# Moving TensorE's load of block numbers, and four of its steps, in a graph layer with a mixture-of-experts FFN

## What is computed

```
def _L0_gnn_ref(x, edge_index, weight, bias):
    summed = jax.ops.segment_sum(x[src], dst, num_segments=n)
    deg = jax.ops.segment_sum(jnp.ones_like(src, dtype=x.dtype), dst, num_segments=n)
    agg = summed / jnp.maximum(deg, 1.0)[:, None]
    out = jnp.concatenate([x, agg], axis=-1) @ weight
    out = out / jnp.linalg.norm(out, axis=-1, keepdims=True)
    return out + bias
...
def _L0_ffn_ref(h, gate_w, gate_b, w1, b1, w2, b2):
    logits = x @ gate_w + gate_b
    probs = jax.nn.softmax(logits, axis=-1)
    idx = jnp.argmax(probs, axis=-1)
    ...
    buf = jnp.zeros((E, C, D), dtype=h.dtype).at[idx, pos_safe].set(x, mode='drop')
    hmid = jax.nn.relu(jnp.einsum('ecd,edf->ecf', buf, w1) + b1[:, None, :])
    ybuf = jnp.einsum('ecf,efd->ecd', hmid, w2) + b2[:, None, :]
...
x = x + _L0_gnn_ref(_layernorm(x, axis=-1), edge_index, L0_gnn_weight, L0_gnn_bias)
x = x + _L0_ffn_ref(_layernorm(x, axis=-1)[None], ...)[0]
```

## Time and profile before

| | |
|---|---|
| timed runs | 1510.32, 1512.84, 1513.54 us; median 1512.84 |
| span of the profiled execution | 1742.4 us |
| TensorE, VectorE, GpSimd busy | 68%, 52%, 53% of the span |
| the main loop in the profiled execution | 156 to 1552 us |

### The profile page before, as it was taken

The page is one execution under the profiler, slowest core; times in us unless marked ns, Lnnn a source line. Parts: engine busy times, 40 slices in busy tenths (PEclk is TensorE's granted clock), DMA queues, the critical chain, the costliest instruction groups (busy, mean ns, idle before and its releaser), DMA issues.

```text
span 1742.4 us, 32300 instructions
## 1 busy us (share of the span) xinstructions
PE 1183.2 (68%) x6813; PEld 838.8 (48%) x6814; DVE 898.6 (52%) x3823; ACT 469.4 (27%) x1362; POOL 922.7 (53%) x939
## 2 busy tenths in 40 slices
PE   0105566677777777777777776877677777777785
PEld 0004444455555555555555554645455655554553
DVE  5753444455555545454555554554555545554443
ACT  2221111122222222222222322223222222233432
POOL 4136656656666656555656655565556665640110
PEclk9998676789999989998989998999998899888998
DMA  7736667554545444544445444444454544431111
GB/s 236 235 134 205 185 215 232 185 160 131 147 136 146 135 131 132 149 121 134 136 118 139 126 138 115 134 127 140 114 143 121 146 120 137 124 103 34 38 42 38
DMA packets 126810, 238.77 MB, mean 137 GB/s; under 512 B 21263, under 2 KB 85126, under 8 KB 126792
## 3 DMA queue, kind: packets, MB, share of 16 engines
q0 software_dynamic: 55808, 160.87, 32.7%
q1 hardware_dynamic: 70984, 77.72, 14.1%
HBM read 207.46 MB, written 39.29 MB: 142 GB/s over the span
## 4 chain that ended last, share of the span: by engine, by line
PE 28%; issue 19%; DVE 17%; another core or an unknown queue 11%; DVEq 10%; DMA 7%; ACT 4%; POOL 2%; SPq 2%; ACTq 0%; POOLq 0%
PE ps_q L684 10%; PE ps_h L747 5%; PE ps_b L766 5%; PE ps_a L738 3%; DVEq L1252 3%; DVEq L1060 2%; DMA ring<-parts_d,idx 2%; DVE sel L991 2%; PE ps_a L725 2%; DMA b_b<-in_L_ffn_b 2%; DMA out<-ys,node_i 1%; PE ps_t L755 1%; DVE acc L1000 1%; ACT cat_t L580 1%
## 5 line engine op out<-in xcount | busy, mean ns | idle before, releaser
L460 POOL DMA_INDIRECT ring<-parts_d,idx x784 | 763.0, 973 | 541.1 <-PE ps_q L684 277.9
L684 PE MATMUL ps_q<-ring,sel 128*128 128x256 bf16 x2928 | 506.0, 299 | 245.0 <-DMA ring<-parts_d,idx 96.7
L684 PEld LDWEIGHTS ps_q<-ring,sel 128*128 128x128 bf16 x2928 | 270.4, 106 | 416.8 <-issue 242.2
L766 PE MATMUL ps_b<-w_sb,hid_t 128*128 x864 | 264.6, 441 | 124.2 <-issue 71.2
L991 DVE SCALAR_TENSOR_TENSOR sel<-lane,block,dst_t 128x512 bf16<-128x512 bf16 x245 | 184.4, 753 | 197.4 <-issue 116.2
L766 PEld LDWEIGHTS ps_b<-w_sb,hid_t 128*128 128x128 f32 x864 | 169.6, 214 | 161.6 <-issue 141.5
L747 PE MATMUL ps_h<-w_sb,hid_t 128*128 x432 | 213.6, 622 | 5.7 <-ACT hid_t L583 5.7
L1000 DVE TENSOR_TENSOR acc<-acc,ps_q 128x257 f32 x245 | 103.3, 422 | 178.3 <-issue 57.3
L690 PE MATMUL ps_q<-ones_bf,sel 128*128 128x1 bf16 x976 | 170.8, 175 | 0.0
L738 PE MATMUL ps_a<-gw_sb,cat_t 128*128 128x256 f32 x416 | 136.3, 459 | 19.3 <-ACT cat_t L580 15.6
L604 ACT ACTIVATE hid_t<-ps_t,b_t 128x128 f32<-128x128 f32 x432 | 117.8, 382 | 55.5 <-remote 40.1
(11 more groups left out here) (180 smaller groups left out, 1296.1 us busy)
## 6 DMA issues: line engine op xcount, KB each, us to landing
w_sb<-in_L_ffn_w SPq DMA_DIRECT2D x32, 512.0 KB
ring<-parts_d,idx POOLq DMA_INDIRECT x784
disp_d<-row SPq DMA_DIRECT2D x1, 8450.0 KB
parts_d<-w_sb SPq DMA_DIRECT2D x6, 1344.0 KB, 5.8
xs<-disp_d SPq DMA_DIRECT2D x55, 130.0 KB
ys<-disp_d SPq DMA_DIRECT2D x55, 130.0 KB
b_b<-in_L_ffn_b SPq DMA_DIRECT2D x55, 128.0 KB
xb<-in_x SPq DMA_DIRECT2D x51, 128.0 KB
```

Of the source, the lines that this page charges most:

```text
L460: pool.indirect_dma_start(ring[:, (k % 2) * TQ + j, :], None, parts_d[:, :], bass.IndirectOffsetOnAxis(ap=idx[:, k * TQ + j:k * TQ + j + 1 ...
L684: mm = pe.matmul(ps[:, 0:D], sel[:, s, j, :], ring[:, (k % 2) * TQ + j, part * D:(part + 1) * D], start=(j == 0 and part == 0), stop=(j == ...
L766: last_ = pe.matmul(ps_b[:, 0:D], hid_t[:, j, :], w2_sb[:, j, ds(expert[0] * D, D)], start=(j == 0), stop=(j == JF - 1))
```

## The change

TensorE's load of the next trip's eight block numbers goes into eight spare registers, `next_regs`, and is moved from behind the first group of the last quad to behind the second half of the first FFN product in the third quad. A new step, `turn_quads`, copies them over at the trip's end. In `plan`, the first half of the first FFN product moves from behind group 2 to behind group 3 of the second quad; what follows in the third quad moves one group later each; `down` 0 and 1 move into the last quad; the transposes of the normalised row move from behind group 3 to behind group 2 of the last quad, and `down` 4 to 7 all stand behind group 3. Nothing else is changed.

```diff
+            next_regs = [pe.alloc_register(f"next_quad_blocks{i}") for i in range(2 * QS)]
...
                 def load_quads():
 
-                    pe.load(regs, qtab[0:1, ds(t * QS + QS, QS), :])
+                    pe.load(next_regs, qtab[0:1, ds(t * QS + QS, QS), :])
+
+                def turn_quads():
+                    for now, then in zip(regs, next_regs):
+                        pe.reg_mov(now, then)
...
                         [steps((node, linear, 0)),
                          steps((node, linear, 1)),
-                         steps((chunk, up, 0)),
-                         steps()],
-                        [steps((prev, counts), (chunk, up, 1)),
+                         steps(),
+                         steps((chunk, up, 0))],
+                        [steps((prev, counts)),
+                         steps((chunk, up, 1), (quads, load_quads)),
                          steps((chunk, hid_transposes, 0)),
-                         steps((chunk, hid_transposes, 1)),
-                         steps((chunk, down, (0, 1)))],
-                        [steps((quads, load_quads), (chunk, down, (2, 3))),
-                         steps((chunk, down, (4, 5))),
-                         steps((chunk, down, (6, 7))),
-                         steps((node, xl_transposes))]]
+                         steps((chunk, hid_transposes, 1))],
+                        [steps((chunk, down, (0, 1))),
+                         steps((chunk, down, (2, 3))),
+                         steps((node, xl_transposes)),
+                         steps((chunk, down, (4, 5, 6, 7)), (quads, turn_quads))]]
```

## The result

The changed kernel takes **1610.59 us** (median of 4 runs, 1608.28 to 1626.81); the kernel before, beside it, 1511.58 (4 runs, 1509.12 to 1513.54). The ratio is **1.067, with a 95% interval of 1.062 to 1.073**: 99 us slower. The forecast had the sign right and the size wrong by a factor of three (+32 us), and 1610 lies outside its range of 1485 to 1590.

The account below looks back on a forecast made before the run. The loop was taken to be bound by VectorE's chain, with ScalarE in its gaps. Load and other shifts counted 0, the new order 0.8 us in each of 40 trips: +32 us on 1512.84 gave 1545 us, range 1485 to 1590.

Parts of the forecast that it names:

- The bound: In the loop: VectorE's chain, with ScalarE in its gaps and TensorE a little ahead, sets the trip at 24.0 us.
- Part 1: TensorE's load behind the first FFN product: its 1.8 us stall falls to 0 to 0.2 us, taken as 0.
- Part 2: Transposes ahead of the last four second FFN products: TensorE waits 2.4 us for ScalarE, next quad starts 1.4 us later.
- s: Start of VectorE's selection for the extra visit, in nearly all trips in the last quad; 842.20 us in the trace before.
- X: End of the normalised row on ScalarE, put at a fixed 8.66 us after s.
- Part 3: How much of the next quad's 1.4 us delay reaches the chain, through the exponential: taken as 0.8 us a trip.
- Rival 3: The wait before the transposes lowers TensorE's clock: 1.9 us in 20 trips, 1583 us; chance 0.17, shared with an unhidden load.
- Rivals 1 and 2: First: TensorE's jitter sets the loop, the wait cushions it, 1459, chance 0.25; second: VectorE's chain hides everything, 1515, chance 0.11.
- The signs set down beforehand: Under 0.3 us idle after the load; 2 to 3 us before the transposes, some 100 in all; next quad X + 2.6 or later.

Follow-up runs that it names:

- e3: Changed kernel with the transposes of the normalised row put last in the trip again, the load left at its new place; 1514.0 us.
- e4: Changed kernel with two unread products issued ahead of TensorE's wait for the normalised row, in trips with a chunk; 1514.0 us.
- e6: Changed kernel with the transposes last again and VectorE's own load of block numbers moved to the trip's end, into spare registers; 1487.9 us.
- e9: Changed kernel, order untouched, with VectorE's own load of block numbers taken off its chain in two halves; 1477.6 us.
- e1: Kernel before with only TensorE's load moved behind the first FFN product, all other steps at their old places; 1526.1 us.
- e7: Kernel before with VectorE's own load of block numbers moved to the trip's end, nothing changed on TensorE; 1505.9 us.
- e2: Changed kernel's order of steps, but TensorE's load left in the last quad, into the old registers; 1528.1 us.
- e10: Kernel before with only TensorE's load moved, plus one unread product ahead of the wait for the normalised row; 1516.3 us.
- e5: Changed kernel with one unread product ahead of TensorE's wait for the normalised row, in trips with a chunk; 1527.4 us.

## Why the prediction was wrong in size

**The bound: right.** The chain of VectorE and ScalarE was put at 24.0 us a trip by taking the overstated waits out of the trace of before. Trips at full clock are 23.7 us (e3) and 24.05 us (e4). Taking work off that chain pays at full clock (0.33 us a trip in e6 against e3, 0.86 in e9 against e4); taking it off TensorE alone doesn't (e1; e6 against e7).

**Part 1, the load: right.** Hidden behind the first FFN product, nothing left at the new place, moves 0.18 us, and worth nothing by itself at full clock. The same 1.8 us came back at the transposes.

**Part 2, the new wait: right in place, too small in length.** The last visit's group started 2.57 us after the selection for the extra visit (837.40, the row below) and not 3.26, so TensorE stood at the transposes at s + 5.7 instead of s + 6.3; X came at s + 8.5 (8.66 predicted). The wait was 2.93 us in the trip shown and 3.1 in the mean, against 2.4. The row of VectorE for s, and of TensorE for that group, in the changed kernel:

```profile
837.40 0.75 DVE L996 SCALAR_TENSOR_TENSOR sel<-lane,block,dst_t 128x512 bf16<-128x512 bf16 x1 [0.32 <-issue]
```

```profile
839.97 0.49 PE L685 MATMUL ps_q<-ring,sel 128*128 128x256 bf16 x3
```

**Part 3, what reaches the chain: the step that failed.** The sum took X + 2.7 for the next quad and X + 5.85 for the exponential, both with TensorE at full clock behind the wait. In the changed kernel they are X + 4.8 and X + 8.4. At full clock (e4) they are X + 2.5 and X + 5.4 (the prediction's own terms, 0.3 + 0.35 + 1.9, make 2.55 and not 2.7): the mechanism of the order was right, with 0.28 us a trip (e4 against e3 at full clock) where 0.8 was taken, and its 32 us are not to be found in e4's time. What failed is the price of the products behind the wait: the sum had them all at full clock and put the clock's part at nothing. That part is 93 us: 3.03 us in each of 24 trips and 1.57 in 13 (the changed kernel less e4).

**Rival 3 is what happened.** It named the mechanism and the row that shows it: 2.16 us of idleness, then a stretch at a granted 0.51. It was given in half the trips, 1.9 us each, and a small chance. It should have been the forecast. The argument against it was that idle times of 1.8 us stand in the last quad of each trip already, and the loop is granted 0.92 all the same. Three things were missed there. A mean of 0.92 leaves room for a fall in some trips, and e2's and e7's rows show one behind 1.90 and 1.95 us. A wait of 2.4 us is longer than the 2.16 after which the fall had been seen, so the 1.8 say little about it. And the price is paid behind the gap: behind the old one stood two products and a quad's remainder with time to spare before X, behind the new one four products, the next quad and the transposes of cat, all in front of the exponential that the chain waits for. With rival 3's own numbers in nearly every trip, 40 x 1.9 = 76 us on top of the order's 0 to 32, the forecast would have been 1589 to 1621, and held the 1610.6. That this comes near is in part luck: the clock falls in 37 trips of 40, and where it falls for all of the 5 us it costs 3.0 us and not 1.9, as the groups and the transposes of cat are slow too.

**Rivals 1 and 2: no.** The kernel is not faster, and something did move. The signs set down beforehand came true: no wait at the load, a wait of 2 to 3 us before the transposes (3.1 in the mean), some 100 us in all (117.5), put down to ScalarE's row, and the next quad later than X + 2.6. They would have looked the same at 1545; the sign that tells the two apart, the granted clock in the 5 us behind X, was not among them.

**Open.** Why e10's clock stays at 0.94 though its wait is down to 0.8 us. And what decides whether the granted clock falls in a given trip: the changed kernel has three trips at full clock behind waits of 3.1 to 3.3 us; in single trips of e5 with 1.9 us and of e1 with 1.65 us it was 1.00 in the 5 us after, while the mean over e1's trips dips to 0.64 about 5 us behind X.

## What to carry to other kernels

Hiding a stall of an engine that is not the bound only moves it to the next place where that engine meets the bound; before moving instructions, ask what will stand right behind the wait that results. For TensorE a recurring wait is priced by its length *and* by its follower: read in the trace behind which waits and in how many trips the granted clock falls, and cost the products behind it at 1.2 GHz, up to what the chain waits for. If such a wait can't be avoided, put it behind the products that others wait for (e3), shorten it from the producer's end (e9), or fill part of it with unread products (e4); then shorten the chain's own load. And compare two kernels trip by trip, sorted by the granted clock, before a difference is put down to a path: e7's 18 us looked like a load on the path and were the clock's.

## What was unexpected of the hardware

- 1.7 us of useless products a trip make this kernel 97 us faster; 0.85 us give 83 of them.
- Behind 2.93 us of idleness the granted clock was 0.50 for the next 5 us, and full behind 1.03 to 1.32 us in the trips shown. The length alone doesn't decide: in the changed kernel the clock stayed at 1.00 behind 3.31 us, and in e7 it fell behind 1.95 us.
- A load of eight 16-bit values into TensorE's registers takes 1.965 us, eight moves between registers 0.178 us. A double set of registers is thus nearly free.
- The mean granted clock of the loop (0.90, 0.95, 1.00) says little about the time: 0.95 (e3) and 1.00 (e4) give the same 1514.0 us.
- A load of 1.97 us in TensorE's sequencer cost nothing in trips at full clock (e7 against e6: 0.00 us over 18 trips), and 1.5 us in each of ten trips in which the clock fell.
